# Extra context rows projected with 32-bit weights and centred as keys, in the opening of a fused cross-attention and feed-forward kernel

## The reference

```python
y_dca = y[:, -DCA:, :]                                    # DCA = 16
y_main = y[:, :-DCA, :]
kv_dca = (y_dca @ Wkv_dca + bkv_dca).reshape(b, DCA, 2, H, HD)
k_dca = _ln(kv_dca[:, :, 0], kn_dca_w, kn_dca_b)          # per head: minus mean, over deviation
v_dca = kv_dca[:, :, 1]
q = _ln((x @ Wq + bq).reshape(b, s1, H, HD), qn_w, qn_b)
...
ctx = _attn(qT, k, v) + DCA_WEIGHT * _attn(qT, k_dca, v_dca)
return ctx @ Wo + bo
...
w = lut[idx]                                              # feed-forward weights, 16 values
```

## Time and profile of the kernel before

| what | value |
|---|---|
| median of three runs | 808.67 us |
| profiled execution, its own time | 808.67 us |
| span of its trace | 806.4 us (2.27 us lie around it) |
| PE busy over the span | 759.6 us, 94% |
| DVE busy | 509.5 us, 63% |
| ACT busy | 492.5 us, 61% |
| POOL busy | 254.5 us, 32% |
| chain that ended last, by engine | PE 81%, DVE 12%, ACT 3%, issue 2%, POOL 1% |

### The profile page before, as it was taken

The page is one execution under the profiler, slowest core; times in us unless marked ns, Lnnn a source line. Parts: engine busy times, 40 slices in busy tenths (PEclk is TensorE's granted clock), DMA queues, the critical chain, the costliest instruction groups (busy, mean ns, idle before and its releaser), DMA issues.

```text
span 806.4 us, 14838 instructions
## 1 busy us (share of the span) xinstructions
PE 759.6 (94%) x5842; PEld 311.6 (39%) x5842; DVE 509.5 (63%) x991; ACT 492.5 (61%) x1001; POOL 254.5 (32%) x267
## 2 busy tenths in 40 slices
PE   2888786999999999999999999999999999999998
PEld 1342232333443343234443343235433433365445
DVE  7979999898877994215769952238499800153211
ACT  3479889788646886663658866636488855511100
POOL 6883221000763321004843320036522200014320
PEclk9998999899999999999999999999999999999999
DMA  7749998586320001222400003222000000100001
GB/s 254 194 126 273 255 261 211 141 185 159 122 68 1 1 2 34 73 53 62 122 4 1 2 23 71 53 66 55 1 1 1 2 27 28 40 14 1 0 14 40
DMA packets 74244, 61.22 MB, mean 76 GB/s; under 512 B 33408, under 2 KB 60800, under 8 KB 73920
## 3 DMA queue, kind: packets, MB, share of 16 engines
q1 hardware_dynamic: 73840, 60.02, 28.0%
q10 hardware_dynamic: 208, 0.26, 0.1%
q0 software_dynamic: 128, 0.00, 0.0%
HBM read 43.29 MB, written 10.55 MB: 67 GB/s over the span
## 4 chain that ended last, share of the span: by engine, by line
PE 81%; DVE 12%; ACT 3%; issue 2%; POOL 1%; DVEq 0%; POOLq 0%; ACTq 0%
PE ps L1677 54%; PE ps L2028 8%; PE ps L2009 6%; PE ps L1980 5%; PE ps L1728 5%; DVE arena L1122 4%; DVE nmax L1472 3%; PE ps L1876 2%; ACT ps L1005 2%; PE ps L2015 2%; DVE nmax L1477 1%; DVE arena L1129 1%; POOL hrstd L684 0%; DVE stat L1159 0%; ACT arena L808 0%
## 5 line engine op out<-in xcount | busy, mean ns | idle before, releaser
L1677 PE MATMUL ps<-arena,wf_hi 128*128 128x512 f16 (+2 forms) x736 | 211.0, 371 | 0.7 <-issue 0.7
L1005 ACT ACTIVATE ps<-ps,nmax 128x496 f32<-128x496 f32 x256 | 166.2, 652 | 23.1 <-DVE nmax L1477 23.1
L1037 ACT ACTIVATE arena<-ps 128x1024 f32<-128x1024 f32 x128 | 124.3, 1026 | 72.1 <-PE ps L2015 72.1
L1677 PE MATMUL ps<-arena,wf_lo 128*128 128x512 f16 (+2 forms) x368 | 136.1, 370 | 0.0
L1677 PE MATMUL ps<-wf_hi,arena 128*128 128x512 f16 (+3 forms) x374 | 114.8, 368 | 0.4
L684 POOL TENSOR_TENSOR hrstd<-hvar,mhalf 128x16 f32<-128x16 f32 (+1 forms) x33 | 101.3, 3086 | 40.5 <-DVE hvar L1226 40.3
L1677 PEld LDWEIGHTS ps<-arena,wf_hi 128*128 128x128 f16 (+1 forms) x736 | 69.6, 100 | 85.6 <-issue 21.6
L1122 DVE TENSOR_SCALAR arena<-arena,wf_lo 128x2048 f16<-128x2048 f16 (+1 forms) x132 | 89.5, 739 | 5.6 <-PE ps L1728 5.4
L633 POOL TENSOR_TENSOR xrstd<-xvar,mhalf 128x1 f32<-128x1 f32 x32 | 23.9, 746 | 206.9 <-DVE xvar L1164 206.9
L1728 PE MATMUL ps<-arena,wf_lo 128*32 128x512 f16 (+1 forms) x1056 | 66.4, 396 | 13.5 <-ACT arena L832 9.5
L1677 PE MATMUL ps<-wf_lo,arena 128*128 128x512 f16 (+3 forms) x187 | 68.5, 366 | 0.0
(11 more groups left out here) (153 smaller groups left out, 1039.9 us busy)
## 6 DMA issues: line engine op xcount, KB each, us to landing
arena<-idx SPq DMA_DIRECT2D x124, 128.0 KB, 3.6
arena<-in_x SPq DMA_DIRECT2D x32, 256.0 KB, 2.9
wf_lo<-in_idx SPq DMA_DIRECT2D x10, 512.0 KB, 5.1
idx<-wf_hi SPq DMA_DIRECT2D x10, 384.0 KB, 4.3
out<-arena SPq DMA_DIRECT2D x15, 256.0 KB, 2.0
wf_lo<-in_idx SPq DMA_DIRECT2D x11, 256.0 KB, 6.3
arena<-in_ctxT SPq DMA_DIRECT2D x5, 512.0 KB, 3.7
v_next<-arena SPq DMA_DIRECT2D x8, 256.0 KB, 4.4
```

What stands on the lines that cost most here:

```text
L1005: last = act.activation(sc, sc, ACT.Exp, bias=nmax[:, 0, t, h:h + 1], accum_out=den[:, 0, t, h:h + 1])
L1037: act.activation(probs[n_ % 2][:, 2 * p:2 * p + 2, :], ps[:, bank:bank + 2, :], ACT.Exp).then_inc(s["probs_set"], 1)
L1677: last = pe.matmul(dst, l, r, start=(first and i == 0), stop=(stop and i == len(todo) - 1))
```

## The change

Five things change, all in the first batch.

1. **Extra rows.** The split of the extra weights and of the extra context rows is gone from DVE and ACT. ACT scales the 128 x 128 block of extra context in place by 256, and the products of unit d and of its values take it and the raw 32-bit weights: two 32-bit matmuls in place of six 16-bit ones, each. DVE `extra_centre` now sums the 32 columns of each head of the projected keys in PSUM and subtracts the mean there; `square` of unit d waits for that.
2. **First chunk ahead of the scores.** The four compares of `one_hot(0)` stood behind the second pair's maximum; they now stand one by one behind the x turn 3, `low_half(3)`, the `kd` copies and `low_half(6)`.
3. **The last query's turn.** `normalise(8)` moves behind the second pair's maximum, `turn_heads(8)` behind the second quad (`scores(2)`), `rescale(8)` behind the second pair's exponentials, into another bank; `look_up(0)` gets a wait for all nine units' `rescale`, `scores(2)` one for eight.
4. **Orders.** The lists of DVE, ACT, PE and POOL in the opening are rewritten: x is standardised earlier and turned later on DVE, value products of the first two tiles stand ahead of `project(2)`, `values_low` stands ahead of `key_low` and both ahead of `context_lo`, `convert(0)` ahead of `rstd(0)`, `convert(1)` behind `rstd(1)`.
5. **SP.** `Wo` is loaded after the last projection and the last value product, just ahead of the next context, and no longer between the first chunks' loads.

```diff
+        turn_bank = lambda u: TB + u % 2 if u < NU else FB + 1
-            sp.wait_ge(s["wd_lo"], 1)
-            sp.dma_start(st_o..., by_chunk("Wo")).then_inc(s["wo_in"], 16)
...
             sp.wait_ge(s["proj_done"], nth_unit((0, 0), len(UNITS_0)))
+            sp.wait_ge(s["v_done"], nth_value((0, 0), len(values_of((0, 0)))))
+            sp.dma_start(st_o..., by_chunk("Wo")).then_inc(s["wo_in"], 16)
...
+            def extra_centre(a):
+                u = units_of(a).index(("d", 0))
+                kd_ps = heads(ps[0:MD, proj_bank(a, u), :])
+                dve.wait_ge(s["proj_done"], nth_unit(a, u + 1))
+                dve.tensor_reduce(sum_d, kd_ps, AX_X, ALU.add).then_inc(s["kd_sum"], 1)
+                dve.wait_ge(s["kd_sum"], 1)
+                dve.scalar_tensor_tensor(out=kd_ps, in0=spread(sum_d), scalar=-1.0 / HD, in1=kd_ps, op0=ALU.mult, op1=ALU.add)\
+                    .then_inc(s["kd_cent"], 1)
...
-                        keys = [(both(lambda a_: cd[a_][:, i, :]), both(lambda a_: wd[a_][:, i, 0:D])) for i in range(KC)]
+                        keys = [(ctx_dca[:, i * MD:(i + 1) * MD], st_d[:, i, 0:D]) for i in range(KC)]
...
+                if not c:
+                    pe.wait_ge(s["tr_hi"], len(UNITS_0))
...
-                        pe.wait_ge(s["tr_hi"], nth_unit(a, len(units)))
+                        pe.wait_ge(s["tr_hi"], nth_unit(a, len(units) - (prev is None)))
...
-                    if prev is None and m == 0:
+                    if prev is None and m == 2:
                         turn_heads(8)
```

More of the change, by code:

```diff
@@ L686, in core @@
                 if prev is None:
+                    norm(1, 0, (0, 0))
+                    norm(1, 1, (0, 0))
+                    selectors()
+                    shift_patterns()
+                    norm(1, 2, (0, 0))
+                    lookup_constants()
+                    norm(1, 3, (0, 0))
+                    convert(0)
                     rstd(0)
-                    convert(0)
-                    for u in range(1, len(units)):
-                        rstd(u)
+                    rstd(1)
                     convert(1)
+                    rstd(2)
+                    rstd(3)
+                    rstd(4)
+                    rstd(5)
+                    rstd(6)
+                    rstd(7)
+                    rstd(8)
                     low_half(a, 7, 0)
@@ L1437, in core @@
-                    parameters()
-                    normalise(a, 1, True)
+                    normalise(a, 0, True)
+                    parameters()
+                    standardise(1, 2, a, x_first[2], x_first[2])
+                    variance(a, 2)
+                    normalise(a, 1, True)
+                    low_half(0)
+                    value_bias()
+                    turn(1, 2, a, LB0[2])
                     variance(a, 3)
-                    extra_low()
                     normalise(a, 2, True)
-                    low_half(0)
@@ L2038, in core @@
                         between(S_TWO + n_)
-            for t in range(2):
-                turn(1, t, (0, 0), LB0[t], x_first[t])
             def prepare(slot):
```

157 lines of the change are left out of this document (67 added, 90 removed).

## The result

The changed kernel takes 811.80 us (median of five runs, 811.64 to 813.11), the kernel before beside it 808.22 us (807.40 to 809.32): 3.6 us slower, ratio 1.0045, 95% interval 1.0034 to 1.0055. The profiled execution took 812.32 us with a span of 810.0, against 808.67 and 806.4 before. PE is busy for 759.1 us of it, as before (759.6): its work is the same, the places are not.

What follows compares the result with a forecast made beforehand. It took POOL's train of powers to lead the opening, DVE to 137 us, then PE. 3.1 (first maximum) + 0 (score head) + 1.65 (clock) = 4.75 us on 808.67 gave 813.4 us, range 808.0 to 815.8.

Steps and rivals of the forecast that it cites:

- the clock holds at 32 us: Rival: PE keeps full clock through its idle time ahead of the value products; 811.8 us, chance 0.13 alone.
- Step 1: First x turn on DVE, behind more low halves: ends at 20.1 us, 2.5 later; bounds 2.0 to 2.6.
- Step 2: First projection on PE: same length, 5.7 us at half clock, 20.15 to 25.9; lower bound 2.7 us less.
- Step 3: Value products wait for the context's low half, ending at 32.0; PE idles 3.1 us, third power starts at 37.8, formerly 33.94.
- Step 7: PE's clock at 32 us: idle time brings half clock to the value products, 1.65 us; bounds 0 to 2.6.
- Step 4: POOL's powers, third to eighth: 2.90 us each, unit d's gap 0.9; first maximum at 58.85, 3.1 us later.
- Step 5: First chunk's four compares, moved into DVE's idle time in the opening: cost nothing; 2.8 us if the train outran DVE.
- Step 6: Last query's turn and first look-up: first to fifth maximum stays 10.9 us, gain zero; 8.9 at full clock.
- Step 8: SP loads Wo ahead of the next context, near 57 us: price 0 to 0.6 us, taken as 0.
- Reaches the end one for one: Premise: PE bounds the kernel from 137 us on, so any earlier gain or loss reaches the end in full.
- gaps below 1 us left it at full: Argument for the rival that PE's clock also holds at the second quad: 809.8 us, chance 0.12.
- worst case for the compares: Each of four early compares on DVE could hold one power's start on POOL: up to 2.6 us more.

Runs made afterwards that it cites:

- e3: Changed kernel with the first x turn (and the bias low half) put back to its earlier place on DVE: 813.86 us, ratio 1.0065 to the kernel before.
- e2: Changed kernel with the context's low half made right behind the first variance on DVE: 810.58 us, ratio 1.0032 to the kernel before.
- e1: Changed kernel with ten unused products filling PE's idle gap ahead of the value products: 812.48 us, ratio 1.0051 to the kernel before.
- b2: Kernel before with only the 32-bit extra rows, all orders kept, Wo issued behind the extra rows' value product: 807.88 us, ratio 0.9996.
- e7: e6 with the four compares of the first chunk put back behind the maxima: 809.10 us, ratio 1.0009 to the kernel before.
- e6: e5 with the last query's normalisation, turn and rescaling put back behind the first quad: 807.92 us, ratio 0.9991 to the kernel before.
- b1: Kernel before with only the load of Wo issued later, after all projections and value products of the opening: 810.01 us, ratio 1.0015.
- e5: e2 with Wo loaded as soon as the extra rows' products are done: 809.82 us, ratio 1.0012 to the kernel before.
- e4: Changed kernel with the last query's normalisation, turn and rescaling put back behind the first quad: 813.35 us, ratio 1.0063 to the kernel before.
- c2: c1 with six unused products on PE ahead of the first projection: 809.36 us, ratio 1.0005 to the kernel before.
- c1: e6 with the opening's four lists on DVE, POOL, PE and ACT laid out anew: 809.72 us, ratio 1.0009 to the kernel before.
- c3: c2 with ACT's list reordered, the second conversion behind the first and the second index store ahead of Wo: 807.59 us, ratio 0.9997 to the kernel before.

## Why the prediction came out as it did

**The outcome.** Forecast 813.4 in 808.0 to 815.8 and slower; measured 811.8. Of the 4.75 us of the sum, 3.6 came. Three sizes were off, and they partly cancelled: the opening 1.3 us less than forecast, the score head 1.2 more, and 0.9 given back at 145 us. That the fifth maximum came 4.65 us late for the sum's 4.75 is luck. The rival "the clock holds at 32 us" gives 811.8, the measured time to the digit, and that is chance too: its condition did not hold, for the granted clock there was 0.52.

**Step 1** (first x turn 2.5 us later): right, 20.04 for 20.1. But it is no cause of the late first maximum: e3 undoes it, and that stays at 59.24.

**Step 2** (first projection at half clock throughout): mis-sized by 1.1 us. It ended at 24.8 for 25.9: twelve products took 4.50 us and not 5.30, the last ones at the faster pace. The pace is read from the products' durations; the granted clock column shows 1.00 from 20.1 to 24.6 us, and so it does over the slow products of the earlier trace rows, so here the clock itself is argued and not shown.

**Step 3** (value products wait for the context's low half): right in mechanism, and e2 shows it to be the cause of the late opening. The low half ended at 30.28 for 32.0: 1.1 us from step 2, and 0.6 because the value low half took 1.22 us, not the 1.85 of the earlier trace rows. That row stands beside a POOL conversion; in the kernel after the conversion ended at 26.08, 0.08 us ahead of the low half. In e3 the two overlap, and it takes 1.87 us (last section), so the 0.6 us hung on a close finish. The idle time was 2.81 us for 3.1.

**Step 7** (the clock): right. Value products 4.44 us against 2.75 is 1.7, forecast 1.65, and e1 takes this away. The other 0.2 us of its 1.90 is an earlier start (30.22 for 30.43).

**Step 4** (the train of powers): right. From the third power's start to the eighth's end 18.6 us for 18.5; unit d's gap 0.74 for 0.9; a 32-bit product 0.88 for 0.86 (two start 1.77 us ahead of the bias product). With steps 2 and 3 the first maximum is at 59.21, where the sum had 58.85 plus 1.65. That DVE's 3.7 us were worth nothing, b2 shows. The step's "DVE waits on this stretch, it does not lead it" holds only for that stretch: ahead of 30 us DVE's list leads, as e2 and e3 show together.

**Step 5** (compares cost nothing there): right, none delayed another engine's step.

**Step 6** (first to fifth maximum 10.9 us, as before): off in size, 12.1. The half clock at the second quad, the turn and the rescaling came as forecast. The step let the fifth maximum follow the last compare; it follows the third quad, which stands behind the whole look-up and took 1.47 us at half clock (69.73 to 71.12). And the step's zero hid two opposite parts: in the kernel with context first and `Wo` early, e7 prices the early compares at a gain of 1.5 us, e6 the last query's move at a loss of 1.7.

**Step 8** (SP at no cost): in the trace of the kernel after no wait shows it: ACT takes the next context at 65.98 us without idle time. But b1 prices the move at 1.2 us in the kernel before, e5 at 1.6. The argument "each chunk is issued a whole chunk ahead of its use" looked at the gathers; what comes late in b1 are the conversions' index loads (7.6 us to landing for 256 KB instead of 6.3, from 56 to 100 us).

**Where the change's time lies, then**, each part put back in this order: context low half 1.1 us (its interval overlaps that of the changed kernel; the 3.3 us in the trace do not rest on it), `Wo` 1.6, last query's turn 1.7. Together they are 4.4 us, more than the 3.6 lost, and what stays of the change, the 32-bit rows, the early compares and the other new orders, makes e6 (0.9991). The shares depend on the order: the last query's turn put back alone (e4) makes the time 1.5 us longer. Which of the other new orders of ACT, PE and POOL gain or lose was not tested one by one.

**"Reaches the end one for one"** was the first premise. Behind 137 us it holds within 0.1 us but for the places named: near 145 us, where the clock decides, and near 400 us in e1. Between 56 and 137 us it does not hold for gains: the 2.9, 3.3 and 2.3 us by which e1, e2 and e4 are ahead of the changed kernel at the fifth maximum were partly or wholly gone by 100 us.

## What to carry to other kernels

When a step moves on a busy in-order queue, follow what each other engine waits for, not how late the moved step is: one 1.2 us operation placed behind three others made the first maximum 3.3 us later, another whose place let PE start 2.1 us later did not move it. A megabyte moved into a stretch where the DMA engines were 0.92 busy cost 1.2 to 1.6 us, though the trace of the changed kernel shows no wait for it. Price changes of 0.2% by medians of many runs, undo them one at a time and in combination, and expect that a gain can be taken back where TensorE idles later on.

## What the runs showed of the hardware that was not expected

**The same idle time, two clocks.** PE waits 2.23 us for the same step in the kernel before, the kernel after, e1 and e5, and the 32 look-up products behind it then take 1.91 us in the first two, 3.12 in e1, 3.58 in e5 (rows above). In the kernel before, that look-up, and one that ran slow (granted 0.56) behind a much shorter idle time:

```profile
70.93 3.31 PE L1728 MATMUL ps<-arena,wf_lo 128*32 128x512 f16 x32 [0.67 <-ACT wf_hi L801]
...
89.05 1.91 PE L1728 MATMUL ps<-arena,wf_lo 128*32 128x512 f16 x32 [2.23 <-ACT arena L832]
```

The granted clock was 1.00 over the look-up at 89.05, 0.59 in e1 and 0.54 in e5. So whether it goes from 2.4 to 1.2 GHz is not told by the length of the gap ahead alone, and the prediction's "gaps below 1 us left it at full" does not hold for the row at 70.93. The step falls at 89.05, 93.66, 90.77 and 89.93 us in the four kernels; what else differs between them no run isolates. The difference is worth 0.9 to 1.7 us each time, as much as most parts of this change. The Trainium skill ("TensorE: Matmul & The Clock Gate", "What's actually happening") says that the activity monitor runs freely and is not reset by a kernel, so that the same work meets it at varying moments; the spread of the runs fits that, and no run here shows the monitor itself.

**Useless work early makes the work behind it faster.** In c2 six idle-time products are followed by the faster pace from 16.3 us on (three products in 0.82 us), and the idle times of 0.4 to 1.3 us between the projection's parts do not lose it again; in c1 the same parts run at about half that pace up to 21 us (1.46 us). The granted clock column reads 1.00 in both, as in all rows ahead of 25 us looked at here, so the clock is inferred from the durations. The gain, 1.25 us at the first maximum, does not show in the medians.

**VectorE and GpSimd slow each other.** A low half of 1024 columns took 1.85 us beside a conversion and 1.22 in the kernel after, where the conversion had just ended. In e3 the conversion ran up to 26.51 us:

```profile
25.72 1.87 DVE L1536 SCALAR_TENSOR_TENSOR wv<-arena,wv 128x1024 f16<-128x1024 f32 x1
```
In e2 it is the power that is longer, 3.82 us beside the low halves and 2.90 right behind:

```profile
26.47 3.82 POOL L684 TENSOR_TENSOR hrstd<-hvar,mhalf 128x16 f32<-128x16 f32 x1 [0.39 <-DVE hvar L1231]
30.51 2.90 POOL L684 TENSOR_TENSOR hrstd<-hvar,mhalf 128x16 f32<-128x16 f32 x1 [0.21 <-DVE hvar L1231]
```

In c3 a standardisation, 0.54 us elsewhere, took 1.75 us beside two conversions:

```profile
30.80 1.75 DVE L1176 TENSOR_SCALAR arena<-arena,mv,xrstd 128x512 f32<-128x512 f32 x1
```

The compares, 0.74 us each, ran during powers and were not stretched; the power at 57.06 beside the last of them took 2.90 us as well. The rule of the Trainium skill that the prediction weighed ("SBUF — State Buffer", "Who interferes with whom") agrees with the first three; its worst case for the compares, 2.6 us, did not come.
